# Three subtractions of the second dense stage on VectorE instead of GpSimd

## What the kernel computes

```python
agg = segment_sum(m * norm[dst][:, None], dst)        # edge stage, done before
h   = h + res * tanh(agg + h @ W_loop + b)            # W_in and W_out are applied to the sums here
mu  = h @ mu_w + mu_b
x   = x + mu                                          # layernorm(x) feeds the experts
```

## Time and profile before

| | us |
|---|---|
| median of 3 runs | 2920.09 (2918.03 to 2920.86) |
| profiled execution, its own time | 2916.88 |
| its span | 2915.1 |
| VectorE busy in it | 2377.0 (82%) |
| GpSimd busy in it | 1928.0 (66%) |

### The profile page before, as it was taken

One profiled execution on the slowest core, in us unless ns is written; L12 is line 12 of the kernel. 1 busy time (PEld: TensorE's weight loads), 2 busy tenths in 40 slices (PEclk: granted clock), 3 DMA queues, 4 the chain that ended last, 5 costly groups with the idle time before them and its releaser, 6 DMA issues. The chain is left out here.

```text
span 2915.1 us, 55660 instructions
## 1 busy us (share of the span) xinstructions
PE 2677.8 (92%) x20716; PEld 2527.6 (87%) x20716; DVE 2377.0 (82%) x3308; ACT 1847.0 (63%) x3125; POOL 1928.0 (66%) x2028
## 2 busy tenths in 40 slices
PE   2799999999999996979999999999999957759998
PEld 1699999999999996979999999999999957759998
DVE  5688888888888887968888888888888869966666
ACT  5676666666666664867766666766666634435543
POOL 3677777777777775557777777777777747742322
PEclk9999999999999998989999999999999979979999
DMA  7433333333333333443333333333333323331222
GB/s 231 137 104 106 107 106 106 107 106 106 106 106 106 106 107 88 152 136 105 106 106 106 107 106 105 107 106 106 106 107 106 106 91 109 112 123 55 65 67 70
DMA packets 163417, 313.21 MB, mean 107 GB/s; under 512 B 34381, under 2 KB 96269, under 8 KB 163189
## 3 DMA queue, kind: packets, MB, share of 16 engines
q0 software_dynamic: 79872, 218.21, 25.9%
q1 hardware_dynamic: 82389, 91.10, 9.6%
q10 hardware_dynamic: 928, 0.85, 0.1%
HBM read 264.16 MB, written 45.88 MB: 106 GB/s over the span
## 5 line engine op out<-in xcount | busy, mean ns | idle before, releaser
L609 PE MATMUL edge_rg<-edge_rel_hi,edge_hot 128*128 128x256 f32 x6656 | 1505.2, 289 | 22.1 <-DVE edge_hot L499 4.8
L609 PE MATMUL edge_rg<-edge_rel_lo,edge_hot 128*128 128x256 f32 x4992 | 1270.2, 283 | 0.0
L609 PEld LDWEIGHTS edge_rg<-edge_rel_hi,edge_hot 128*128 128x128 f32 x6656 | 1185.5, 192 | 80.8 <-DVE edge_hot L499 63.7
L432 POOL DMA_INDIRECT edge_xg<-h,src x832 | 788.4, 948 | 266.7 <-issue 218.1
L432 POOL DMA_INDIRECT edge_xg<-emb,src x832 | 789.1, 948 | 262.8 <-issue 222.1
L609 PEld LDWEIGHTS edge_rg<-edge_rel_lo,edge_hot 128*128 128x128 f32 x4992 | 957.2, 192 | 0.1
L449 ACT CAST edge_m_hi<-edge_rg 128x1024 fp32r<-128x1024 f32 x416 | 422.8, 1016 | 488.1 <-DVE edge_rg L508 488.1
L514 DVE TENSOR_TENSOR edge_m_lo<-edge_rg,edge_m_hi 128x1024 fp32r<-128x1024 f32 x416 | 509.6, 1225 | 223.5 <-ACT edge_m_hi L449 223.5
L456 ACT ACTIVATE edge_hot<-edge_typ,minus_type 128x512 fp32r<-128x512 f32 x832 | 527.0, 685 | 178.9 <-PE edge_typ L599 174.8
L499 DVE TENSOR_SCALAR edge_hot<-edge_typ,type_of 128x512 fp32r<-128x512 f32 x832 | 582.6, 742 | 7.7 <-ACT edge_hot L456 7.7
L508 DVE TENSOR_TENSOR edge_rg<-edge_xg,edge_rg 128x1024 f32<-128x1024 f32 x416 | 510.8, 1228 | 67.1 <-DMA edge_xg<-emb,src 19.6
(11 more groups left out here) (160 smaller groups left out, 3797.7 us busy)
## 6 DMA issues: line engine op xcount, KB each, us to landing
edge_xg<-emb,src POOLq DMA_INDIRECT x832, 2.7
edge_xg<-h,src POOLq DMA_INDIRECT x832, 2.8
set_x_rows<-in_x SPq DMA_DIRECT2D x25, 256.0 KB, 3.7
emb<-set_e_rows SPq DMA_DIRECT2D x25, 256.0 KB, 3.4
emb_t<-set_e_t SPq DMA_DIRECT2D x25, 256.0 KB, 2.9
dense_prev<-emb_t SPq DMA_DIRECT2D x25, 256.0 KB, 2.8
h_t<-dense_work SPq DMA_DIRECT2D x25, 256.0 KB, 2.0
h<-dense_work SPq DMA_DIRECT2D x25, 256.0 KB, 2.1
```

The source lines that it names most:

```text
L432: pool.indirect_dma_start(xg[:, GROUP * q + t, :], None, nodes, bass.IndirectOffsetOnAxis(ap=at, axis=0)).then_inc(gathered[q], 16)
L609: ins = pe.matmul(rg[q % 2][:, t, :], hot[:, q % 2, c, t * P:(t + 1) * P], part[:, c, :], start=(c == 0 and part is rel_hi), stop=(c == FULL))
```

## The change

The three subtractions `previous_low`, `h_low` and `columns_low` leave GpSimd's list and join VectorE's, with the same lags. GpSimd keeps `inverse_deviation` and `add_bias`. VectorE's list is also in another order: `scaled_low` stands directly behind `residual`, `h_low` and `previous_low` come next, `moments` behind them, then `scale`, `normalize` and at the end of the turn `columns_low`. The dense stage of layer 0 (`first` true) stays as it is.

```diff
             def inverse_deviation(c, b, n, d, m):
...
-            def columns_low(c, b, n, d, m):
-
-                pool.wait_ge(cols_done, copies(c))
-                pool.wait_ge(cols_hi, c + 1)
-                pool.tensor_tensor(part(1, c), cols, part(0, c).bitcast(F32),
-                                   ALU.subtract).then_inc(cols_lo, 1)
-
-            def h_low(c, b, n, d, m):
-                pool.wait_ge(h_hi, c + 1)
-
-                wait_past(pool, mu_done, c)
-                pool.tensor_tensor(h_parts[1][:], h_t[:, b], h_parts[0][:].bitcast(F32), ALU.subtract).then_inc(h_lo, 1)
-
-            over_chunks(pool, (3, h_low), (4, inverse_deviation), (1, previous_low), (3, add_bias),
-                        (5, columns_low), deep=DEEP)
+            over_chunks(pool, (4, inverse_deviation), (3, add_bias), deep=DEEP)
 
         @block.vector
...
+            def previous_low(c, b, n, d, m):
+
+                dve.wait_ge(prev_hi, c + 1)
+
+                wait_past(dve, lin_done, c - 1)
+                dve.tensor_tensor(prev_parts[1][:, b], prev[:, d], prev_parts[0][:, b].bitcast(F32),
+                                   ALU.subtract).then_inc(prev_lo, 1)
...
+                dve.tensor_tensor(part(1, c), cols, part(0, c).bitcast(F32),
+                                   ALU.subtract).then_inc(cols_lo, 1)
...
+                dve.tensor_tensor(h_parts[1][:], h_t[:, b], h_parts[0][:].bitcast(F32), ALU.subtract).then_inc(h_lo, 1)
...
             else:
-                over_chunks(dve, (3, residual), (4, moments), (1, scaled_low), (4, normalize), (0, scale),
-                            (1, weights_low), deep=DEEP)
+                over_chunks(dve, (3, residual), (1, scaled_low), (3, h_low), (1, previous_low), (4, moments), (0, scale),
+                            (4, normalize), (1, weights_low), (5, columns_low), deep=DEEP)
```

More of the change, by code:

```diff
@@ L920, in normalize, with columns_low, h_low @@
                 ins.then_inc(rows_done, 1)
+            def previous_low(c, b, n, d, m):
[3 more added lines that the diff above has]
+                                   ALU.subtract).then_inc(prev_lo, 1)
+            def columns_low(c, b, n, d, m):
+                dve.wait_ge(cols_done, copies(c))
+                dve.wait_ge(cols_hi, c + 1)
+                dve.tensor_tensor(part(1, c), cols, part(0, c).bitcast(F32),
+                                   ALU.subtract).then_inc(cols_lo, 1)
+            def h_low(c, b, n, d, m):
+                dve.wait_ge(h_hi, c + 1)
+                wait_past(dve, mu_done, c)
+                dve.tensor_tensor(h_parts[1][:], h_t[:, b], h_parts[0][:].bitcast(F32), ALU.subtract).then_inc(h_lo, 1)
             def weights_low(c, *place):
```

## The result

| | median us | runs |
|---|---|---|
| before | 2919.06 | 4 (2916.88 to 2920.86) |
| changed | 2940.02 | 4 (2936.37 to 2941.65) |

The changed kernel is slower: ratio 1.007, interval 1.0053 to 1.0088, or +21.0 us where 22 were predicted. Its profiled execution took 2936.37 us, which is 19.5 more than that of the kernel before, and its span is 2934.6.

What follows compares the result with a forecast made beforehand. VectorE was taken to set the second dense stage's pace; twenty full turns at +0.96 us (+19.2) and the ends (+2.9) give +22.1, 2939.0 on the profiled execution, 2942 predicted for the median, range 2927 to 2956.

Steps and rivals of the forecast that it cites:

- The wait for ScalarE, 1.34 a turn: VectorE, `scaled_low` directly behind `residual`: nothing covers ScalarE's rounding of h and then the sums, costing 1.34 us a turn.
- `scale` free, -1.07: VectorE's `scale`: only small GpSimd instructions remain beside it, so its step falls from 2.28 to 1.21 us, -1.07 a turn.
- `normalize` keeps one neighbour, -0.97: VectorE's `normalize`: one GpSimd neighbour goes, `add_bias` stays; the pair's step falls from 2.59 to 1.62 us, -0.97 a turn.
- Three subtractions at 0.61: Three 128x512 subtractions added on VectorE, 0.61 us each with GpSimd idle: +1.83 us a turn, up to 0.5 more.
- `normalize` 8.05 to 8.3 behind `residual`: Start of `normalize` in VectorE's new turn: 8.05 us by the inverse deviation's readiness, 8.30 if 2.48 behind L910; 8.1 taken.
- the lower bound: The earlier estimate for `normalize`: 8.05 us behind the start of `residual`, with L910 at 5.82.
- The turn: One full turn of VectorE in the second dense stage: 10.35 us against 9.39, +0.96; twenty full turns give +19.2.
- The ends, +2.9: Start and drain of the stage: +1.2 us at turn 5, +2.3 from turn 25, -0.6 for the last `columns_low`.
- TensorE doesn't bind: TensorE in the second dense stage: VectorE sets the pace; TensorE becoming the bound was a rival at chance 0.08.
- the third rival: TensorE becomes the bound at its lower clock: turn 11.4 us, another 1.05 for 20 turns, 2963 us; chance 0.08.

Runs made afterwards that it cites:

- sums_rounded_first: The changed kernel with ScalarE rounding the scaled sums ahead of h; 3321.9 us, 9.4 us faster than the kernel before in its set (3331.3).
- bias_tiny: The changed kernel with GpSimd's `add_bias` on 128x2 elements only, other columns left out; 3329.3 us, -1.9 us against the kernel before in its set (3331.3).
- moments_ahead: The changed kernel with `moments` back between `residual` and `scaled_low` on VectorE; 3309.2 us, 22.1 us faster than the kernel before in its set (3331.3).
- bias_beside_moments: moments_ahead with GpSimd's `add_bias` waiting for its chunk's `residual` and ahead of the inverse deviation; 3284.0 us, 13.5 us faster than the kernel before in its set.
- bias_beside_moments_x4: bias_beside_moments with four buffers for x instead of two and x loaded earlier; 2872.8 us, 48.8 us faster than the kernel before in its set (2921.6).
- moments_ahead_x4: moments_ahead with four buffers for x and the earlier load, the bias left in place; 2900.9 us, 20.7 us faster than the kernel before in its set.

## Why the prediction was right

By its own steps, with what the changed kernel's trace has for each:

- **The wait for ScalarE, 1.34 a turn.** `scaled_low` starts 1.98 us behind `residual` with 1.24 idle (2.00 and 1.25 were predicted from turn 3). sums_rounded_first took off 30.5 us, where 1.34 for 22 turns and 1.05 in turn 3 are 30.5. Right, and shown; that the two agree to the tenth is chance, since the interval of the comparison is some 4 us to either side.
- **`scale` free, -1.07.** 1.26 us for the pair, against 2.36. Right.
- **`normalize` keeps one neighbour, -0.97.** 1.67 us for the pair, with the bias begun 0.06 us earlier. Right, and bias_tiny shows what is left in it: 23 us were predicted as 21.
- **Three subtractions at 0.61.** Steps of 0.61, 0.60 and 0.60, lengths of 0.68. Right.
- **`normalize` 8.05 to 8.3 behind `residual`.** 7.96 in this turn. `normalize` came 2.18 us behind L896, a little under the 2.23 of the lower bound: GpSimd's first small instruction began 0.49 us behind L896 (2401.57), where before it stood behind the subtraction of h and began 0.68 us behind L910 (2387.22).
- **The turn.** 10.15 in the turn shown, and 10.31 in the mean of 20, against 10.35. That the mean comes so near is in part luck. The turn shown is one of those that are written out, and by these the sum was 0.2 too long (`normalize` 0.14 earlier than taken, the rest in steps of some hundredths). The turns of the loop take 10.27 and, the first of each pass of four, 10.57. Before, the loop had 9.34 and 9.53 in the same places. In the 10.27 turns `scale` begins about 0.08 us later behind L896 (0.41 instead of 0.33), and in the 10.57 turns the wait for ScalarE is about 1.55 and not 1.24 (`scaled_low` at 2417.90 and 2459.27). The prediction had no term for the loop, and I haven't tested what makes it longer.
- **The ends, +2.9.** The start was over-sized: TensorE began 1.04 us later (1.35 predicted, though the prediction's own 2362.8 - 2361.53 is 1.27), with the subtraction of chunk 0 at 2358.42 and not 2358.7; turn 4 came at 2375.50 (2375.95), turn 5 at +0.6 us (+1.2). The drain from turn 25 to the last transposes was 27.4 us (27.5), against 25.2 before.
- **TensorE doesn't bind.** Its mean granted clock did fall in this stage, from 0.92 to 0.83, as the third rival had it and as the page "TensorE: Matmul & The Clock Gate" of the Trainium skill ("Why this matters for your kernels") warns of gaps between bursts. But its gaps before the transposes stayed (54.8 us for 21 turns). VectorE sat idle for no matmul in that stretch:

```profile
engine line waited for: us in total, times, longest us
...
ACT dense_work L1044 <- PE dense_lin L142: 48.0, 22, 3.8
DVE dense_scaled L772 <- ACT dense_scaled L1017: 27.4, 21, 1.6
DVE dense_work L904 <- POOL dense_rstd L855: 14.9, 22, 1.1
```

(waits in the changed kernel from 2380 to 2600 us). ScalarE waits for TensorE, but in time that it has: in sums_rounded_first the time fell by the whole of the other wait.

So the sum came out for its reasons. On the profiled executions it was 22.1 predicted and 19.5 measured: 0.7 us too much for the turns, 0.6 for the start, under 0.1 for the drain, and about 1.3 that the experts' stage gave back (below), for which the prediction had no term. The medians differ by 21.0, and so look nearer than the sum of the terms was. The rule on the shared port, that a VectorE instruction with two inputs in SBUF is blocked for the whole of a GpSimd instruction that reads SBUF and began first, is in the Trainium skill, "SBUF — State Buffer", section "Who interferes with whom". The traces agree: `scale` is 2.39 beside the bias and 1.28 without, and `moments`, whose instructions have at most one input in SBUF, is not longer beside it. The number of inputs isn't all: `normalize` has one large input in SBUF and is held too (1.67 against 0.73 us), and no run here varies what makes the difference.

## What to carry to other kernels

Moving work to the engine that sets the pace can pay, if it takes an equally costly collision away. The exchange itself is small here: by the prediction's terms, 1.83 us of work a turn replaced 2.04 us of being held. About half of what moments_ahead gained (10.6 of 20.4 us in the 24 turns, between sums_rounded_first and moments_ahead) came from the other thing that the moved work did there, which was to fill the time until the inverse deviation was ready. What decided the sign was the order written with it, which put the waiting instruction directly behind the one that its producer waits for too. Read the lists of both engines side by side: between an instruction and the one that needs another engine's answer to it, the other engine's time must be filled with independent work. And before moving an instruction earlier, ask when its data land and not only when its engine is free.

## What was unexpected of the hardware

- An instruction of GpSimd stretches too when VectorE is ahead of it: in moments_ahead the bias, begun 0.02 us behind VectorE's `previous_low` (2869.55 and 2869.53), took 1.83 us (bias_beside_moments: 1.84), and beside `moments` 1.31. Both engines lose in such a collision.
- The experts' stage gave about 1.3 us back: TensorE's first matmul of it came 20.8 us later than before (2637.03 against 2616.26) but the span grew by 19.5. In the changed kernel the matmuls there run at the higher clock level (0.12 us apart instead of 0.21) after 2.9 us (2637.03 to 2639.94), before after 5.9 us (2616.26 to 2622.16). That is one execution of each, and neither chance nor another cause of the 1.3 us is excluded.
- The mean granted clock of TensorE from 2400 to 2530 us was lowest where its waits before the transposes were longest: 0.83 with waits of up to 4.2 us (changed), 0.92 with up to 2.7 (before), 1.00 with 0.8 (bias_beside_moments_x4). It doesn't follow the longest wait alone, since moments_ahead_x4 has 0.92 with up to 1.9. No cost of the lower clock shows in this stage: in all four VectorE set the pace.
